# Twenty unread products put into three waits of TensorE in a fused feed-forward, attention, feed-forward kernel

## The reference, cut to what matters

```python
x = x + 0.5 * ffn(layernorm(x))      # 8 experts, each token to its argmax expert, 128 -> 512 -> 128
x = x + attn(layernorm(x))           # rms norm of q and k, rope, softmax over 256 keys, projection
x = x + 0.5 * ffn(layernorm(x))
```

## Time and profile before

| | us |
|---|---|
| median of three runs | 490.5 |
| lowest, highest | 489.43, 491.69 |
| span of the profiled execution | 487.4 |
| TensorE busy in it (matmuls) | 432.1 |
| VectorE busy | 382.9 |
| ScalarE busy | 348.6 |
| GpSimd busy | 349.7 |

### The profile page before, as it was taken

The page is one execution under the profiler, slowest core; times in us unless marked ns, Lnnn a source line. Parts: engine busy times, 40 slices in busy tenths (PEclk is TensorE's granted clock), DMA queues, the critical chain, the costliest instruction groups (busy, mean ns, idle before and its releaser), DMA issues.

```text
span 487.4 us, 14012 instructions
## 1 busy us (share of the span) xinstructions
PE 432.1 (89%) x4108; PEld 321.3 (66%) x4108; DVE 382.9 (79%) x1055; ACT 348.6 (72%) x782; POOL 349.7 (72%) x561
## 2 busy tenths in 40 slices
PE   8988999989878899999989998897887979799994
PEld 5348999767665555565655555565554569689994
DVE  4885778887887898988989898988678557877772
ACT  4416777768647898989998998897577746556761
POOL 8028898878766988688784776499736607899885
PEclk9898999999998999999999999999599779999999
DMA  7872335251100000000000000000001122223210
GB/s 201 268 263 60 92 82 152 62 174 38 34 21 16 13 20 9 13 12 13 9 9 3 3 3 3 3 19 20 24 19 36 34 63 68 78 79 91 70 32 6
DMA packets 28649, 27.02 MB, mean 55 GB/s; under 512 B 5684, under 2 KB 25947, under 8 KB 28018
## 3 DMA queue, kind: packets, MB, share of 16 engines
q1 hardware_dynamic: 24034, 17.65, 12.2%
q0 software_dynamic: 4544, 8.49, 6.3%
HBM read 16.56 MB, written 12.71 MB: 60 GB/s over the span
## 4 chain that ended last, share of the span: by engine, by line
PE 40%; DVE 19%; POOL 15%; issue 13%; ACT 7%; DMA 2%; DVEq 1%; POOLq 0%; ACTq 0%
DVE Smax L1756 8%; PE PS L860 7%; PE PS L1001 6%; PE PS L876 6%; PE PS L954 5%; POOL out L630 5%; PE PS L977 4%; POOL Unread L601 3%; PE PS L936 3%; ACT Pt L1218 3%; DVE St L1375 2%; DMA Pt<-rows,TokI 2%; PE PS L920 2%; ACT QkT L1122 2%; PE PS L913 2%
## 5 line engine op out<-in xcount | busy, mean ns | idle before, releaser
L1756 DVE TENSOR_REDUCE Smax<-PS 128x4 f32<-128x1024 f32 x128 | 155.8, 1224 | 35.3 <-PE PS L954 34.5
L1218 ACT ACTIVATE Pt<-PS 128x1024 f32<-128x1024 f32 x128 | 126.4, 1024 | 19.9 <-PE PS L977 16.6
L876 PE MATMUL PS<-W,HsT 128*128 x624 | 86.3, 282 | 7.5 <-DVE Ys L1627 3.1
L860 PE MATMUL PS<-XsT,Ws 128*128 128x128 f32 x624 | 86.1, 283 | 2.2 <-ACT XsT L1122 2.0
L876 PEld LDWEIGHTS PS<-W,HsT 128*128 128x128 f32 x624 | 76.6, 193 | 12.8 <-issue 11.6
L860 PEld LDWEIGHTS PS<-XsT,Ws 128*128 128x128 f32 x624 | 79.3, 198 | 5.4 <-ACT XsT L1122 2.9
L1001 PE MATMUL PS<-Pt,Vg 128*32 128x256 f32 x1024 | 72.2, 401 | 0.2
L954 PE MATMUL PS<-QkT 24*128 24x256 f32 x512 | 60.9, 311 | 2.6 <-DVE Smax L1756 1.7
L703 POOL TENSOR_TENSOR HL<-Rn,Zero 128x512 fp32r<-128x512 f32 x28 | 35.3, 1282 | 38.4 <-DVE Rn L1739 36.9
L608 POOL DMA_INDIRECT Pt<-rows,TokI x39 | 40.4, 1036 | 31.3 <-DVE TokI L1573 19.8
L601 POOL MEMSET Unread<- 128x352 f32 (+1 forms) x140 | 62.0, 443 | 0.2
(11 more groups left out here) (255 smaller groups left out, 721.0 us busy)
## 6 DMA issues: line engine op xcount, KB each, us to landing
AtCol<-slots SPq DMA_DIRECT2D x39, 65.5 KB, 1.9
rows<-XX SPq DMA_DIRECT2D x8, 288.0 KB, 4.3
XX<-x SPq DMA_DIRECT2D x8, 256.0 KB, 4.6
W<-w1T SPq DMA_DIRECT2D x2, 1024.0 KB, 6.2
W<-w2T SPq DMA_DIRECT2D x2, 1024.0 KB, 9.3
mid<-mid_second SPq DMA_DIRECT2D x1, 1472.0 KB
mid<-Ys SPq DMA_DIRECT2D x16, 64.0 KB
QkT<-NmaxT SPq DMA_DIRECT2D x64, 4.0 KB
```

Source lines behind the costliest of these rows:

```text
L860: last = nc.tensor.matmul(PS[:, h_bank(n) + c // 2, (c % 2) * P:(c % 2 + 1) * P], Ws[:, n % R_WS, c * P:(c + 1) * P], XsT[:, n % 2, :], st ...
L876: last = nc.tensor.matmul(PS[:, y_bank(n), 0:P], HsT[:, n % 2, c, :], W2[:, ds(e * D_FF + c * P, P)], start=(c == 0), stop=(c == FC - 1))
L1218: nc.scalar.activation(Pt[:, m % 2, 2 * pair:2 * pair + 2, :, :].rearrange("p h c t -> p (h c t)"), PS[:, score_bank(m, pair):score_bank(m ...
L1756: nc.vector.tensor_reduce(Smax[:, b % 2, :, at:at + 33:32].rearrange("p t h -> p h t"), PS[:, max_bank(m, pair):max_bank(m, pair) + 2, :]. ...
```

## The change

Twenty more calls of the unread product are made, at three places of TensorE's program. Nothing else is changed.

- Step 50: after the second half of `max_scores` and ahead of `qk_transpose`, TensorE waits until VectorE has normalised the output of sequence 11 (which stood in bank 7) and then multiplies 5 unread products into bank 7.
- Step 58: in `small`, after the wait for a free bank and ahead of the transposition of the last sequence's maxima, 6 unread products go into the bank that the transposition then writes (bank 7).
- After step 64: ahead of `experts(1)`, 9 unread products go into bank 3.

```diff
+FILL_TURN, FILL_MAXIMA, FILL_END = {50: 5}, {58: 6}, 9
...
-            def fill_const(count):
+            def fill_const(count, bank=7):
                 for _ in range(count):
-                    nc.tensor.matmul(PS[:, 7, :], Col[:, :, 0], Col[:].rearrange("p c i -> p (c i)").unsqueeze(1).to_broadcast([P, 2, 2 * P]),
+                    nc.tensor.matmul(PS[:, bank, :], Col[:, :, 0], Col[:].rearrange("p c i -> p (c i)").unsqueeze(1).to_broadcast([P, 2, 2 * P]),
                                      start=True, stop=True)
...
             def small(n):
...
+                if n in FILL_MAXIMA:
+                    fill_const(FILL_MAXIMA[n], bank_of("nmaxT", seq(n, 2)))
                 if seq(n, -5) >= 0:
                     y_transpose(seq(n, -5))
                 if seq(n, 2) >= 0:
                     max_transpose(seq(n, 2))
...
             def step(n):
...
                 if group(n + MAX_LEAD):
                     max_scores(n + MAX_LEAD, 1)
+                if n in FILL_TURN:
+                    pe.wait_ge(*emptied("yb", seq(n - 1, -5)))
+                    fill_const(FILL_TURN[n])
                 if group(n + QKT_LEAD) and n >= 0:
                     qk_transpose(n + QKT_LEAD)
...
             for n in range(RAMP_END, TAIL):
                 step(n)
+            fill_const(FILL_END, 3)
             experts(1)
```

## The result

The changed kernel takes 483.27 us (median of 20 executions, 479.63 to 490.29) against 490.2 us before (20 executions, 485.04 to 493.72): a ratio of 0.9857, with a 95% interval of 0.983 to 0.9884. The forecast was 483.8. The times in us are medians of all executions, while the ratios with their intervals, here and in the table, leave out the slow ones, over 1.5% above their kernel's fastest (six of these twenty). Seven of the twenty took 486.8 to 490.3 us, at a mean granted clock of 0.961 to 0.974, where the other thirteen had 0.975 to 0.995: the clock was still lost somewhere in them. The profiled execution took 481.70 us with a span of 479.7, so 2.0 us lie around the span.

A forecast was written before the change was run, and what follows sets the result against it. The prediction took TensorE at halved clock, behind three waits, as the bound. Gains of 3.2 (step 50), 1.4 (step 58) and 2.1 us (first tiles), with products costing 0, made 490.5 - 6.7 = 483.8 us, range 482.0 to 488.6.

The forecast's parts named there:

- What bounds: TensorE is the bound where its clock is halved, behind three waits of 1.26, 1.38 and 2.15 us.
- Price of a product: An unread product takes 0.216 us at full clock, about 0.42 at the kernel's start; price 0 in all three waits.
- Step 50: Five products in the transposes' wait keep the clock through steps 51 and 52: gain 3.2 us, bounds 2.5 and 3.9.
- counterpart steps 39 and 40: Nearest full-clock steps with the same place in their sequence, 8.22 us, taken as the usual length of steps 51 and 52.
- Step 58: Six products at the last maxima's transposition; lot 2's last six stores leave back to back: gain 1.4 us, bounds 0 and 2.0.
- First tiles: Nine products ahead of the second feed-forward; its first two tiles run at full clock: gain 2.1 us, bounds 0.7 and 3.1.
- The sum: 3.2 + 1.4 + 2.1 = 6.7 us off 490.5, the profiled span of 487.4 with 3.1 us around it: 483.8 us.
- (a): One of the three gains missing: step 50's dip unusual (487.0 us) or one dip returning (485.9); 485 to 487.5, chance 0.24.
- (b): Clock falls all the same or other work is late; at most one small term left: 488.5 to 490.5 us, chance 0.17.
- short waits for VectorE are harmless: By the Trainium skill's rule, two of the three waits are harmless and only the last term is left: 488.4 us.
- (c): Slower: clock already halved at the products, which hold back 3.7 us of work in the three waits: 494.2 us, chance 0.03.

The follow-up runs named there:

- eight columns: Changed kernel with its twenty products at the same places, each streaming 8 columns in place of 512: 488.9 us, 1.0012 against the kernel before.
- step 58 only: Changed kernel with only the 6 products of step 58 left: 486.02 us, 0.991 against the kernel before.
- step 50 only: Changed kernel with only the 5 products of step 50 left: 482.84 us, 0.9858 against the kernel before.
- elsewhere: Changed kernel with its twenty products moved to steps 38 (9), 42 (6) and 46 (5), none in the three waits: 487.41 us, 0.9975 against before.
- 50 and 58: Changed kernel with the products of steps 50 and 58 kept and none at the end: 483.38 us, 0.9853 against the kernel before.
- end only: Changed kernel with only the 9 products ahead of the second feed-forward left: 488.95 us, 0.9995 against the kernel before.
- doubled: Changed kernel with 10, 12 and 18 products in place of 5, 6 and 9: 484.4 us, 0.9927 against the kernel before.
- most: Changed kernel with products in further waits, 13 at the end and 1 behind the second feed-forward's first transposition: 481.25 us, 0.9801 against the kernel before.
- transposes: Changed kernel with 10, 12 and 18 transposes of the identity in place of the products: 485.77 us, 0.9909 against the kernel before.
- more: Changed kernel with products in further waits (first feed-forward's start, steps 0 and 51) and 12 at the end: 481.78 us, 0.9868 against the kernel before.

## Why the prediction was right

- **What bounds.** Right for steps 50 and 58: a dip behind a wait of 1.3 to 1.4 us, TensorE the bound in it, and "eight columns" shows that it is work in the wait that keeps the clock. For the first tiles the dip is right as a reading of that profile; that it is the usual case is not shown.
- **Price of a product.** Right: 0.216 us each; five end before VectorE's reduction lets the transposes go, six push the transposition by 0.09 us, of which step 59's wait of 0.32 us for VectorE takes all, nine end in the wait. The wait at the end grew to 388.17 - 385.25 = 2.92 us, 2.8 forecast. The first price, 0.42 us, was read where the view has the granted clock at 1.00 (2 to 4 us): at the very start that column is no guide, the products' own length is. That the price falls while only such products run is not in the earlier trace rows; in the trace the clock rises at about 21.1 us, behind products from 17.50 and from 20.50 on with seven short counts between them.
- **Step 50.** 3.2 forecast, 3.47 measured. The counterpart steps 39 and 40 were a good row; they carry projections that 51 and 52 lack, as the upper bound said.
- **Step 58.** 1.4 forecast, 1.5 measured, but not of the same parts. The six stores do leave back to back, in 7.79 us and not 7.65: 1.25 us. From step 53 on (349.69, before 353.30: 3.61 us earlier) the first of the six gains another 4.08 - 3.61 = 0.47 us, which the forecast had only in its upper bound. And 0.23 us are lost from the fetch to the transposition (2.55, before 2.32).
- **First tiles.** 2.1 forecast, 2.54 measured between the two profiles: the walk through VectorE's and ScalarE's evacuations was too cautious. That the nine products bring it is not shown: alone they brought 0.4 us of the median, and three of six profiles without them have the first tiles as short.
- **The sum.** 6.7 forecast; 7.6 between the profiles, 6.9 between the medians. What stands around the span in 72 executions of the kernel before is 1.75 to 1.87 us and not 3.1, so the profiled one was an execution of about 489.2 us, a little below the median.
- **Not foreseen.** The sum treats one profiled execution as all of them, and the three gains as independent. The medians say otherwise: step 50 alone 6.5 us, step 58 alone 3.4, the end alone 0.4, all three 6.9. The profiles bear out the lengths of steps 51 and 52 and of the stores one by one, that of the first tiles not; which dips an execution has is different from one to the next. The forecast was right in its terms for the profiled pair. That their sum also lies 0.2 us from the change of the medians is in part luck: alone, steps 50 and 58 brought more than twice their terms in the median, and the end next to nothing.
- **Rivals.** (a) in its first form, that step 50's dip is not the usual one, is the opposite of what was found: step 50 brings the most. Its second form, a dip that returns, may be what seven of the twenty executions show; where they lost the clock isn't known. (b) falls with the result and with "eight columns", and with it the prediction's reading that short waits for VectorE are harmless: the clock fell behind waits of 1.26 and 1.38 us. (c), products at half clock in the three waits, was seen in no profile.
- **Slips.** In (c) the first excess is 2.1 - 1.26 = 0.8, so the sum is 3.6 and not 3.7. The chances of the forecast, of (a) and of the rest alone make 0.80, where 0.79 is given for faster with part of (b) in it. Neither moves the forecast.

**What stays open.** Why the end alone brings nothing measurable and step 50 alone as much as all three. It could be that a dip at step 50 makes the later two likelier, by moving them in time; that is not shown: the profiles without products at the end have the first tiles long with a dip at step 50 (before, eight columns), but also short with one (step 58 only), and without one both short (step 50 only, elsewhere) and long (50 and 58). Dips ahead of the change add to it: the profile of end only began step 50 3.45 us later than before by them. More profiles of the same kernel would be needed.

## What to carry to other kernels

Where the granted clock falls in the profile, look for the wait ahead of it: a wait of little over 1 us can cost 3 to 4 us behind it, and unread products that just fill the wait cost next to nothing (0.09 us at most here). Choose their number by the wait's length at the price of one at full clock, write them into a bank that is free by an order that stands already, and use full products: the same number of products with 8 columns did nothing, and with transposes the one profile still lost the clock behind two of the three waits. Judge it by many executions and their mean granted clock; one profile tells the size of each term and not how often it occurs.

## What the runs showed of the hardware that was not expected

The time from the last store's start to the start of the fetch that waits for its landing differed between profiles: 2.53 to 2.73 us in ten of the fourteen (383.07 to 385.62, 2.55 us, in the changed kernel; 2.54 before), but 3.51 in "doubled", 3.52 in "most", 3.98 in "transposes" and 4.17 in "more". In "more" that gives back 1.6 us of what the clock wins. GpSimd's last store and SyncE's fetch there:

```profile
380.98 0.97 POOL L622 DMA_INDIRECT slots<-XX,SlotI  x1 [0.17 <-issue]
...
385.15 10.57 SPq L535 DMA_DIRECT2D AtCol<-slots  x11
```
